# Finer value-table loads between key loads, a new order of the last expert loads, and two later key-splitting blocks in a one-core perceiver kernel

## The reference, cut to what matters

```python
x = x + L0_ffn(layernorm(x))                       # top 2 of 16 experts, each 256 -> 2 x 256 -> 256, and a shared one
x = x + L1_xattn(layernorm(x), ctx_2048, ctx_2048) # 16 heads of width 16, causal mask of 128 queries on 2048 keys
```

## Time and profile before

| | |
|---|---|
| median of 3 runs | 1075.42 us (1073.46 to 1076.70) |
| the profiled execution | 1077.47 us |
| its span, from first to last instruction | 1075.7 us (1.8 us less than its time) |
| TensorE busy | 1003.9 us, 93% of the span |
| VectorE, ScalarE, GpSimd busy | 707.2, 500.3, 239.5 us |
| DMA over the whole span | 116.66 MB, mean 108 GB/s |

### The profile page before, as it was taken

The page is one execution under the profiler, slowest core; times in us unless marked ns, Lnnn a source line. Parts: engine busy times, 40 slices in busy tenths (PEclk is TensorE's granted clock), DMA queues, the critical chain, the costliest instruction groups (busy, mean ns, idle before and its releaser), DMA issues.

```text
span 1075.7 us, 23419 instructions
## 1 busy us (share of the span) xinstructions
PE 1003.9 (93%) x9600; PEld 797.7 (74%) x9600; DVE 707.2 (66%) x1352; ACT 500.3 (47%) x889; POOL 239.5 (22%) x361
## 2 busy tenths in 40 slices
PE   8999899797999989999989899999999999999886
PEld 3755675365676557776765789999999999999764
DVE  3746357485785568888546686776666576776467
ACT  3242222364676268888665533433333233331475
POOL 4731517020231000000012421210010133332030
PEclk9999999998999999999999999999999999999999
DMA  9761979757654234000131000131111122100000
GB/s 377 316 242 73 327 268 359 285 164 185 164 145 158 84 137 155 1 2 2 51 147 40 1 1 21 41 118 40 44 56 40 53 67 70 60 21 11 2 2 11
DMA packets 42202, 116.66 MB, mean 108 GB/s; under 512 B 4592, under 2 KB 13296, under 8 KB 40432
## 3 DMA queue, kind: packets, MB, share of 16 engines
q1 hardware_dynamic: 38192, 103.56, 28.4%
q0 software_dynamic: 2752, 9.44, 2.5%
q10 hardware_dynamic: 1152, 2.16, 0.5%
HBM read 99.94 MB, written 15.20 MB: 107 GB/s over the span
## 4 chain that ended last, share of the span: by engine, by line
PE 65%; DVE 11%; issue 3%; ACT 2%; SPq 2%; DMA 1%; POOL 1%; ACTq 0%; POOLq 0%; DVEq 0%
PE ps L2598 11%; PE ps L2555 10%; PE ps L1740 6%; PE ps L2112 6%; PE ps L2453 4%; PE ps L2442 4%; PE ps L1900 3%; PE ps L2103 3%; PE ps L1911 3%; PE ps L433 2%; PE ps L1748 1%; DMA arena<-experts_in 1%; SPq L554 1%; PE ps L2462 1%; DVE arena L2749 1%
## 5 line engine op out<-in xcount | busy, mean ns | idle before, releaser
L2598 PE MATMUL ps<-arena 128*128 128x129 f32 x1024 | 126.6, 276 | 1.7 <-DVE xn L2785 1.7
L2598 PEld LDWEIGHTS ps<-arena 128*128 128x128 f32 x1024 | 119.6, 191 | 2.5 <-ACT arena L2704 2.1
L2038 DVE TENSOR_REDUCE st<-ps 128x1 f32<-128x512 f32 x128 | 82.5, 686 | 27.5 <-PE ps L1900 25.7
L2737 DVE TENSOR_REDUCE probT<-ps 128x128 f32<-128x1024 f32 x64 | 82.6, 1290 | 22.0 <-PE ps L2555 12.9
L2215 DVE CUSTOM_DVE_ANT_0 arena<-ps,arena 128x1024 f32<-128x1024 f32 x64 | 75.8, 1222 | 21.7 <-PE ps L2103 18.4
L2704 ACT ACTIVATE arena<-arena 128x1024 f32<-128x1024 f32 x64 | 71.1, 1111 | 27.4 <-DVE arena L2749 27.4
L2677 ACT COPY w<-ps 128x128 f32<-128x128 f32 x32 | 8.5, 265 | 160.1 <-PE ps L2564 160.1
L1985 ACT ACTIVATE arena<-ps 128x1024 f32<-128x1024 f32 x64 | 65.7, 1029 | 36.0 <-PE ps L1911 35.0
L2749 DVE TENSOR_TENSOR arena<-ps,probT 128x1024 f32<-128x1024 f32 x64 | 79.6, 1286 | 1.1
L2112 PEld LDWEIGHTS ps<-const,arena 128*128 128x128 f32 x512 | 54.8, 141 | 31.5 <-issue 24.3
L170 POOL TENSOR_SCALAR small<-small 128x4 f32<-128x4 f32 (+1 forms) x44 | 13.3, 303 | 285.6 <-DVE small L2492 152.8
(11 more groups left out here) (515 smaller groups left out, 2017.7 us busy)
## 6 DMA issues: line engine op xcount, KB each, us to landing
arena<-ctxT_in SPq DMA_DIRECT2D x28, 512.0 KB, 4.1
arena<-experts_in SPq DMA_DIRECT2D x15, 768.0 KB, 6.1
arena<-experts_in SPq DMA_DIRECT2D x15, 512.0 KB, 8.6
key_parts<-w POOLq DMA_DIRECT2D x16, 384.0 KB, 6.6
arena<-key_parts SPq DMA_DIRECT2D x32, 192.0 KB, 3.3
arena<-blocks_in SPq DMA_DIRECT2D x6, 768.0 KB, 19.7
arena<-ctx_in SPq DMA_DIRECT2D x2, 2176.0 KB, 25.1
arena<-early_values SPq DMA_DIRECT2D x4, 1088.0 KB, 11.9
```

Of the source, the lines that this page charges most:

```text
L2038: dve.tensor_reduce(self.mx[:, u % 2, n:n + 1], k.ps[:, n % 2, :], AX.X, ALU.max).then_inc(s("reduced"), 1)
L2598: last = pe.matmul(k.ps[:, 7, 0:DH + 1], self.prob(u)[:, ch * P:ch * P + P], v, start=(ch == 0), stop=(ch == MC))
L2737: dve.tensor_reduce(self.largest[:, h * P:(h + 1) * P], bank.rearrange("p (c t) -> p t c", t=P), AX.X, ALU.max).then_inc(s("c3_max"), 1)
```

## The change

Three things are done. (1) In `found_sync` the up parts of round 7 are issued ahead of the down parts of round 5. (2) GpSimd splits blocks 14 and 15 inside `Causal.gpsimd`, behind the masks and a wait for the up matmuls of round 5; SyncE accordingly waits for the scratch's third quarter at u = 16 and for its fourth at u = 24, and no longer ahead of u = 2. (3) Tables 2 and 3 are loaded in three pieces of 5 chunks (340 KB) each, as entries of `later` behind `factors`: one piece behind the keys of each of u = 11 to 16. `ffmask` then goes with u = 17 to 24 and `w1` with u = 25 to 30. The counts that TensorE waits for follow.

```diff
         seven = self.load_numbers(sp, 7)
+        self.load_found_up(sp, dram, 7, seven)
         self.load_found_down(sp, dram, 5, five)
-        self.load_found_up(sp, dram, 7, seven)
...
-    BEFORE_MLSTM, BEFORE_MLP, BEFORE_EXPERTS = 6, 8, 12
+    BEFORE_MLSTM, BEFORE_MLP, BEFORE_EXPERTS, BEFORE_CAUSAL = 6, 8, 12, 14
...
         pool.sem_inc(s("masks"), 1)
+        pool.wait_ge(k.s("block_up"), 6 + 6)
+        split.gpsimd(pool, o, split.BEFORE_CAUSAL, len(split.BLOCKS))
         pool.wait_ge(k.s("l0_proj"), 6 + ROUNDS)
...
-    def reload_values(self, sp, q, ctx):
-        k, (b, c), n = self.k, divmod(q, DC), (MC - 1) * VH
-        lo = q * MC * VH
-        sp.dma_start(k.vv[:, lo:lo + n], ctx[b][:, c * MC * VH:c * MC * VH + n]).then_inc(k.s(f"context_values{c}"), 16)
+    def values_piece(self, q, ctx, first, end):
+        k, (b, c) = self.k, divmod(q, DC)
+        lo, at, n = q * MC * VH + first * VH, (c * MC + first) * VH, (end - first) * VH
+        return k.vv[:, lo:lo + n], ctx[b][:, at:at + n], f"context_values{c}"
...
-            self.reload_values(sp, q, ctx)
-        for slot in range(2):
-            sp.wait_ge(k.s(f"split_out{slot}"), 8 * len(Split.BLOCKS))
+            to, source, loaded = self.values_piece(q, ctx, 0, MC - 1)
+            sp.dma_start(to, source).then_inc(k.s(loaded), 16)
         sp.wait_ge(k.s("l0_proj"), 6 + ROUNDS)
         for u in range(2, 32):
             if u >= 4:
                 sp.wait_ge(*self.at("keys_queries", 2 * (u - 3)))
+            if u in (16, 24):
+                for slot in range(2):
+                    sp.wait_ge(k.s(f"split_out{slot}"), (96, 128)[u == 24])
             self.load_keys(sp, u)
-            if u in (8, 12):
-                self.reload_values(sp, u // 4, ctx)
...
-                pe.wait_ge(k.s(f"context_values{u // 8 % DC}"), 32 + u // 16 * 16)
+                pe.wait_ge(k.s(f"context_values{u // 8 % DC}"), 32 + u // 16 * 48)
...
             later = parts(k.big[:, 8192:12288], dram["factors"], 4096, "factors_in")
+            later += [n1.values_piece(q, dram["ctx"], 5 * i, 5 * i + 5) for q in (2, 3) for i in range(3)]
             later += parts(k.big[:, 0:B * M], dram["ffmask"], B * M, "ffmask_in")
```

More of the change, by code:

```diff
@@ L1807, in steps_of_second, with gpsimd @@
             yield lambda: self.spread(pool.tensor_copy, 1, parts, i)
-    def gpsimd(self, pool, o):
+    def gpsimd(self, pool, o, split):
         k, s = self.k, self.s
@@ L3331, in _ @@
             pool.wait_ge(s("block_up"), 7)
-            split.gpsimd(pool, o, split.BEFORE_EXPERTS, len(split.BLOCKS))
-            n1.gpsimd(pool, o)
+            split.gpsimd(pool, o, split.BEFORE_EXPERTS, split.BEFORE_CAUSAL)
+            n1.gpsimd(pool, o, split)
             pool.wait_ge(s("a_product"), 32)
```

## The result

| | before | after |
|---|---|---|
| median of the runs | 1076.06 us (4 runs, 1073.46 to 1076.84) | 1063.16 us (4 runs, 1062.77 to 1064.84) |
| profiled execution, its span | 1077.47, 1075.7 us | 1064.84, 1063.0 us |

The ratio after to before is 0.9881, 95% interval 0.9856 to 0.9907: faster by 12.9 us (10 to 15.5). The forecast was 1061, range 1057 to 1067.

What follows compares the result with a forecast made beforehand. TensorE, 93% busy, bounds the kernel, so only its gaps and low-clock work can be won. Tables 11.4 + experts 3.3 = 14.7 us, less 0.2: 1077.47 becomes 1063, or 1061 as median; range 1057 to 1067.

Steps and rivals of the forecast that it cites:

- the "issue" waits: Causal scores: 9.1 us in five TensorE waits; those at passes 9 and 13 put down to keys queued behind 1020 KB tables.
- the gap was not handed on: Rival, 12%: passes 12 to 17 each wait like pass 17, 6.2 us, plus one clock fall, 1.7 us; time 1068.
- the experts' part was not empty: Rival, 12%: late writes and table 0 replace what was removed, so the experts bring nothing; about 1064 us.
- the rival with more gain: Rival, 12%: the pass-17 gap goes too and nothing waits in the experts; 1058 us.
- the wait of pass 17: Causal attention: a 1.03 us gap with only a 256 KB piece beside the keys of u = 17.
- signs of being wrong: Gaps over 1 us at passes 12 to 17, up 7 starting past 195, or a new gap behind 330 us.
- Tables in pieces: Causal attention: removing both 1020 KB transfers wins 11.9 us, less 0.5 for six 340 KB pieces: 11.4 us.
- The loss is 9.47 - 3.22 = 6.25 in pass 9 and 8.9 - 3.22 = 5.7 us in pass 13: Causal attention: time passes 9 and 13 lose against a 3.22 us pass without a gathering step, 11.9 us together.
- The charge of 0.5 us for the pieces: Key loads at u = 11 to 16: six larger pieces cost 0.3 us each, mostly covered; bounds 0 and 6.2 us.
- The sentence that no row shows a cost per DMA adding up: Key parts of 64 KB, issued 0.6 us apart, each land 3.1 us later, against a fixed-cost estimate of 8 us more.
- Experts: 3.3 forecast: End of the experts: up 7 at 192.5, down 5 at 195.6, down 7 at 201.2, 3.3 us ahead; bounds 1.5 and 5.
- Nothing new behind 330 us: After the attention: everything is released by compute and moves as a block, with no new gap.

Runs made afterwards that it cites:

- e3: Kernel before with only the up parts of round 7 issued ahead of the down parts of round 5: 1072.9 us, ratio to before 0.9975.
- e4: Kernel before with only GpSimd's blocks 14 and 15 split and written later: 1076.6 us, ratio to before 1.0012.
- e8: Changed kernel with all four of blocks 12 to 15 behind up 5: 1066.9 us, ratio to before 0.9895.
- e1: Kernel before with only tables 2 and 3 in six pieces behind the keys of u = 11 to 16: 1067.2 us, ratio to before 0.9926.
- e6: Changed kernel with tables 2 and 3 whole, alone beside the keys of u = 11 and 12: 1066.3 us, ratio to before 0.9894.
- e2: Kernel before with up 7 ahead of down 5 and blocks 14 and 15 later, tables still whole: 1071.8 us, ratio to before 0.9965.
- e9: Changed kernel with tables 2, 3 and factors behind u = 3, w1 and ffmask behind u = 31: 1064.7 us, ratio to before 0.9897.
- e10: Changed kernel with all four of blocks 12 to 15 behind up 4: 1062.7 us, ratio to before 0.9874.
- e5: Changed kernel with tables 2 and 3 in two pieces each (544 and 476 KB) instead of three: 1066.6 us, ratio to before 0.9894.
- e11: Changed kernel with the changes of e9 and e10 together: 1063.8 us, ratio to before 0.9892.

## Why the prediction was right, and where its sizes were off

**What bounds, and the sign: right.** The 4.3 us at up 7 were a matter of bytes ahead of it in the queues (e3, e4, e8: each removal of bytes ahead of it moved it), and the "issue" waits were the keys of u = 9 and 13 behind the tables (e1 takes the gaps away, e6 moves them to the passes behind the moved tables). The first two rivals did not come: the gap was not handed on (passes 12 to 17 lost 0.3 us together, where the forecast charged 0.5 and that rival 6), and the experts' part was not empty (2.1 us, and 3.1 in e2). Of the rival with more gain one half came, the wait of pass 17 going, though by chance: it is 0.4 to 0.6 us in e1, e9 and e10. The other half, no waits in the experts, did not come. The waits at passes 26 and 30, 0.6 us each, are no more than with no piece at all beside the keys (0.8 and 0.9 in e9). One of the prediction's signs of being wrong came literally: up 7 starts at 195.70 us, past 195. But this execution reached the experts 2.6 us later, and the same code gave 193.3 in e2, which started 1.2 us later.

**Tables in pieces: 11.4 forecast.** Between the two profiles it is 10.9; but the term took the gaps of one execution as the price of the tables. In e2, e3 and e4 the same transfers cost 8.2 to 9.7 us, and in the timed runs of e1 8.0 (5 to 11). The step that was off is "The loss is 9.47 - 3.22 = 6.25 in pass 9 and 8.9 - 3.22 = 5.7 us in pass 13": right for that execution (11.9 us), where passes 8, 9, 12 and 13 lost 7.9 us in e2, 8.1 in e3 and 10.0 in e4. The gaps there were 0.5 to 1.9 us longer than in e2 and the low stretches twice as long as in all three. A term about 3 us too large would by itself explain why 1061 was 2 us too low; the totals scatter too much to show that it was the reason. The forecast was built on one execution with long gaps and a long low clock; how long they were in it was chance, and it had not allowed for that.

**The charge of 0.5 us for the pieces** was fair: passes 12 to 17 lost 0.3 us in the changed kernel, 1.5 in e1 and 2.0 in e10 with the same pieces, but 1.2 in e9 with none. The wait of pass 17, left in the sum as it was, shrank to 0.1 us, while small waits at passes 4, 18, 22, 23 and 30, of 0.2 to 0.6 us, came up elsewhere; the forecast had no reason for such waits. The sentence that no row shows a cost per DMA adding up stood: with fewer DMAs, in e5 and e6, the attention was not shorter. Its reason was misread: what is issued 0.6 us apart are the three parts of one unit, of 192, 128 and 64 KB; those of 64 KB are a pass apart. They overlap all the same, as each takes some 3.1 us to land. The Trainium skill's "DMA: Bandwidth & Descriptors", section "Anatomy of one DMA", gives its formula for a single DMA issued from GpSimd, while these are issued from SyncE. By that formula as the prediction used it, an estimate, the pieces would have cost 8 us more; the measured attention of 117.7 to 119.5 us decides against using it for transfers that overlap.

**Experts: 3.3 forecast, 2.1 in the profile, 3.1 in e2, 3.8 us timed (1.5 to 6.0).** Counted from the first up matmul, up 7 was forecast at 31.9 us, down 5 at 35.0, down 7 at 40.6. The changed kernel has 32.55, 36.22 and 41.82; e2, the same code there, has 31.53, 35.30 and 40.89. So the working with bytes was right to half a microsecond (it left out VectorE's relief, 0.45 us, through which TensorE stands ready for up 7 that much earlier), and the profiled execution of the changed kernel had its last rounds 0.9 to 1.0 us later than e2. That lateness shows first at the last up part of round 6, which landed 25.9 us behind up 0 there and 24.7 to 25.5 us in the five others with the same code. What delayed it is open. The clock held at 1.00, as forecast. The writes were issued at 192.06 and 197.43; less the 2.6 us by which everything started late, that is 189.5 and 194.8, against 189.8 and 195.0.

**Nothing new behind 330 us**: right, apart from the clock's low stretches, which come and go there in kernels whose code is the same (371 us in before, 362 in e1, 360 in e8, 357 in e10, none in e2).

## What to carry to other kernels

A load that is not urgent, issued ahead of one that is, costs what its bytes take beyond the slack of the urgent one, and then once more if the gap lets TensorE's clock fall; cut it until a piece fits into the slack of one pass (here 340 KB did, 1020 KB did not, and 544 KB can't be told from 340), or put it where the queues are idle. In a stretch in which the DMA engines are full, order the loads by first use and move everything else out of it, writes of other engines too; but look where the engine that makes them works instead, since beside VectorE it can cost more than the bytes gave. Take the price of a gap from several executions before forecasting a gain from it: here the same two transfers cost 7.9 to 11.9 us in four executions.

## What was not expected of the hardware

- Packets of the instruction queue go with most of the waits left in e9: 16 KB on one DMA engine, and a 64 KB load beside it lands 0.9 us later on average (3.67 against 2.81 us). In the changed kernel, with pieces in flight, the difference is 0.2 us (3.50 against 3.28). It is a correlation only.
- The gap alone does not tell what the clock does. Gaps of 1.6 and 1.4 us one pass apart (e6) and one of 2.3 us at up 7 (e3) left it at 1.00; gaps of 1.9 (e11, pass 4) and of 2.4 and 2.5 us (e2) let it fall. It was low for 3.4 us at gaps of 2.0 to 4.9 us (e2, e3, e4), and for 6.8 at gaps of 4.3 and 3.0 (before).
- VectorE beside GpSimd: 0.29 to 1.20 us for one scaling of 128 x 256, 0.69 to 1.79 for two copies in bf16 (e8).
